# Graph blocks with the state stored points-first: aggregate p before the weights are applied, high parts of p before low parts

## The reference

```python
for i in range(NUM_BLOCKS):                          # 4 blocks
    shortcut = points
    p = _lrelu(points)
    g = _group_point(p, idx_t)                       # the 8 nearest
    c = jnp.einsum('oi,bin->bon', w_center[i], p)
    gn = jnp.einsum('oi,bikn->bokn', w_neighbor[i], g)
    points = (c + gn.sum(axis=2)) / (K + 1.0) + shortcut
...
agg = jnp.einsum('bnkc,bnk->bnc', xk, att)           # 30 nearest, softmax weights
return x + agg.transpose(0, 2, 1)
```

## Time and profile before

| | |
|---|---|
| median of 3 runs | 747.92 us (745.57 to 748.06) |
| profiled execution | 747.99 us, its span 746.1 us |
| TensorE busy | 720.4 us, 97% of the span |
| VectorE, ScalarE, GpSimd busy | 80%, 40%, 35% |
| granted TensorE clock, mean | 0.991 of 2.4 GHz |
| gram stage | 0 to 136.2 us |
| block loop | 136.2 to 614.7 us |
| slots 8 to 15 of the eight iterations begin at | 167.4, 221.2, 272.3, 347.6, 415.1, 466.7, 517.7, 571.3 us |
| attention and last store | 614.7 to 746.1 us |

### The profile page before, as it was taken

The page is one execution under the profiler, slowest core; times in us unless marked ns, Lnnn a source line. Parts: engine busy times, 40 slices in busy tenths (PEclk is TensorE's granted clock), DMA queues, the critical chain, the costliest instruction groups (busy, mean ns, idle before and its releaser), DMA issues.

```text
span 746.1 us, 13230 instructions
## 1 busy us (share of the span) xinstructions
PE 720.4 (97%) x5530; PEld 595.1 (80%) x5530; DVE 596.6 (80%) x884; ACT 302.0 (40%) x505; POOL 258.6 (35%) x207
## 2 busy tenths in 40 slices
PE   6999999969999999999999999999998998999998
PEld 4789888858888887888888788888887886777776
DVE  4699999969799999989977979668566777878731
ACT  7436847536634343113302353563552223333210
POOL 2238986955607327203620460651530000000000
PEclk9999999989999999999999999999999999999999
DMA  9612030020002013464300000000000000001001
GB/s 352 215 2 114 1 114 0 1 113 0 1 19 95 2 67 122 164 212 171 125 2 0 1 1 0 1 1 0 1 0 1 2 1 15 30 30 37 36 29 57
DMA packets 21180, 39.88 MB, mean 53 GB/s; under 512 B 10112, under 2 KB 10112, under 8 KB 20864
## 3 DMA queue, kind: packets, MB, share of 16 engines
q1 hardware_dynamic: 20976, 36.93, 14.2%
q10 hardware_dynamic: 144, 2.10, 0.8%
HBM read 32.59 MB, written 6.42 MB: 52 GB/s over the span
## 4 chain that ended last, share of the span: by engine, by line
PE 83%; DVE 8%; POOL 4%; ACT 2%; issue 2%; DMA 1%; SPq 0%; POOLq 0%; DVEq 0%; ACTq 0%
PE bank L1498 31%; PE bank L1477 7%; PE bank L1478 7%; PE bank L1479 7%; PE bank L1522 5%; PE bank L1632 5%; PE bank L1582 4%; PE bank L1633 4%; PE bank L1634 4%; PE bank L1385 2%; PE bank L1387 2%; PE bank L1386 2%; DVE vals L940 2%; DVE idx L942 1%; POOL more L440 1%
## 5 line engine op out<-in xcount | busy, mean ns | idle before, releaser
L1498 PE MATMUL bank<-nbr,pts_l 128*128 128x512 f32 x1024 | 240.9, 393 | 0.4 <-DVE pts_l L978 0.4
L1498 PEld LDWEIGHTS bank<-nbr,pts_l 128*128 128x128 f32 x1024 | 191.7, 189 | 40.5 <-DVE pts_l L978 0.9
L725 ACT CAST pts_l<-bank 128x512 fp32r<-128x512 f32 x64 | 37.6, 588 | 163.5 <-PE bank L1479 163.4
L1477 PE MATMUL bank<-wT,pts_h 128*128 128x512 f32 x256 | 101.2, 395 | 0.0
L1478 PE MATMUL bank<-wT,pts_h 128*128 128x512 f32 x256 | 99.9, 390 | 0.0
L1479 PE MATMUL bank<-wT,pts_h 128*128 128x512 f32 x256 | 99.8, 390 | 0.0
L483 POOL TENSOR_TENSOR scratch<-scratch,q_all 128x512 f32<-128x512 f32 x32 | 43.5, 1365 | 112.1 <-ACT q_all L711 112.1
L986 DVE SCALAR_TENSOR_TENSOR X<-bank,X 128x512 f32<-128x512 f32 x64 | 44.1, 689 | 45.6 <-PE bank L1498 44.5
L834 ACT CAST nbr<-bank 128x512 fp32r<-128x512 f32 x64 | 37.5, 588 | 99.1 <-PE bank L1582 99.1
L1385 PE MATMUL bank<-pts_h 128*128 128x512 f32 (+2 forms) x192 | 70.0, 364 | 7.4 <-DVE pts_l L918 7.4
L488 POOL TENSOR_TENSOR pts_h<-scratch,pts_h 128x512 fp32r<-128x512 f32 x56 | 76.5, 1371 | 0.0
(11 more groups left out here) (209 smaller groups left out, 1324.4 us busy)
## 6 DMA issues: line engine op xcount, KB each, us to landing
more<-a_rows SPq DMA_DIRECT2D x17, 480.0 KB, 4.0
scratch<-a_rows SPq DMA_DIRECT2D x15, 480.0 KB, 4.3
X<-in_ctx SPq DMA_DIRECT2D x12, 512.0 KB, 7.0
out_dram<-X SPq DMA_DIRECT2D x16, 256.0 KB, 2.0
more<-in_ctx SPq DMA_DIRECT2D x4, 512.0 KB, 7.0
scratch<-in_fside_BxSxS SPq DMA_DIRECT2D x2, 1024.0 KB, 12.6
w_keep<-wT SPq DMA_DIRECT2D x1, 2048.0 KB, 6.9
X<-in_x SPq DMA_DIRECT2D x2, 1024.0 KB, 6.2
```

The source lines that it names most:

```text
L1477: pe.matmul(bank[g % 3][:], p_h[:, t, cols], wT[:, 0, t, :], start=(t == 0), stop=False)
L1498: mm = pe.matmul(bank[3 + g % 3][:], y[:, m, t * P:(t + 1) * P], nbr[b][:, m, hf * HALF:(hf + 1) * HALF], start=(m == 0 and part_ == 0), s ...
```

## The change

The host hands x and `fside` over transposed and the state X is stored with points on the partitions (128 points, 512 channels). With this:

- A block is computed as (A + I) p first, then the weights. Slots 0 to 7 are now `aggregate` (16 matmuls, operands p and `nbr`), evacuated by ACT `q_high` and DVE `q_low`; slots 8 to 15 are `wp` (12 matmuls, q and W), and DVE's `x_update` follows those. The number of matmuls is the same.
- Every aggregation unit runs its 8 products with p_h first, then the 8 with p_l. Unit 0 of an iteration waits for p_h and then for p_l piece by piece.
- The 8 pieces of p for the next iteration are issued in slots 8 to 15 as before. These are now the wp slots, and the first piece waits for the aggregation to end.
- `w_turn` and `turn_x` are gone. The split of W runs from SBUF (ACT `w_high`, POOL `w_low`), the second weights are loaded again at g = 32 instead of kept; the split of X for the attention reads X directly.
- The norms of batch 1 come from the diagonal of its gram blocks (`gram_diagonal`, POOL), so `norms(1)` moves to the end of the gram stage and POOL's `add_norm` of tiles 8 to 13 behind it; 8 squares and 7 adds are gone.
- Gram blocks 3 and 11 take two pieces of 320 columns in place of 256 and 512.
- `STEPS_AT` and `ADJ_AT` are shifted; selection ends at g = 43, lookups, network begin one slot earlier; the spreads still begin at g = 121.
- In `attend` the attention weights are the stationary operand and X is the moving one.

```diff
-    PIECES = [((min(t, 2) * P, HALF, 0), (HALF, N, 1)) if t < 4 else ((min(t, 6) * P, N, 1),) for t in range(NT)]
+    CUTS = (HALF, HALF, HALF, 704)
+    PIECES = [((t * P, CUTS[t], 0), (CUTS[t], N, 1)) if t < 4 else ((min(t, 6) * P, N, 1),) for t in range(NT)]
...
-        ADJ_AT = {4: (8, 9), 8: (10, 11), 11: (12, 13), 14: (14, 15)}
+        ADJ_AT = {3: (8, 9), 6: (10, 11), 8: (12, 13), 12: (14, 15)}
...
+            def gram_diagonal(T):
+                cols = slice((T - NT) * P, (T - NT + 1) * P)
+                pool.wait_ge(s_gc, pieces_done(T))
+                if T == NT:
+                    pool.wait_ge(s_sqmm, NH)
+                pool.affine_select(out=diag_g[:, cols], in_=score[T][:, cols], compare_op=ALU.is_equal, fill=0.0,
+                                   base=0, pattern=[[-1, P]], channel_multiplier=1).then_inc(s_dg, 1)
...
-                if 0 < n < N2 and n % (2 * CT) == 0:
-                    act.wait_ge(s_wm, NT * it)
+                if 0 < n < N2 and m == 0:
+                    act.wait_ge(s_m, 2 * CT * it)
...
             def aggregate(g):
                 it, j = g // (2 * CT), g % (2 * CT)
...
-                for m in range(NT):
-                    if j == 0:
-                        pe.wait_ge(s_yl, NT * it + m + 1)
-                    for part_, y in enumerate((y_h, y_l)):
-                        mm = pe.matmul(bank[3 + g % 3][:], y[:, m, t * P:(t + 1) * P],
+                    pe.wait_ge(s_ql, g - 2)
...
+                for part_, p in enumerate((p_h, p_l)):
+                    for m in range(NT):
+                        if j == 0:
+                            pe.wait_ge(s_p1 if part_ else s_p0, NT * it + m + 1)
+                        mm = pe.matmul(bank[g % 3][:], p[:, m, t * P:(t + 1) * P],
...
+            def wp(g):
+                it, m = g // NT, g % NT
+                hf, cols = m // CT, slice(m % CT * P, (m % CT + 1) * P)
+                hi = 0 if it < 2 else 1
+                if m % CT == 0:
+                    pe.wait_ge(s_ql, 2 * CT * it + CT * (hf + 1))
...
             for it in range(ITS):
+                for j in range(2 * CT):
+                    aggregate(2 * CT * it + j)
+                    side(16 * it + j)
                 for m in range(NT):
-                    if 16 * it + m > S0:
-                        spread(2 * (16 * it + m - S0) - 2)
+                    if 16 * it + NT + m > S0:
+                        spread(2 * (16 * it + NT + m - S0) - 2)
                     wp(NT * it + m)
-                    side(16 * it + m)
-                for j in range(2 * CT):
...
-                    aggregate(2 * CT * it + j)
-                    side(16 * it + NT + j)
+                    side(16 * it + NT + m)
```

477 lines of the change are left out of this document (197 added, 280 removed).

## The result

The changed kernel takes **785.95 us** (median of 4 runs, 783.84 to 789.21), the kernel before 747.89 beside it (745.57 to 748.06): ratio 1.052, 95% interval 1.047 to 1.057. Slower, as forecast, but by 38 us and not by 17, and outside the range of 752 to 778. The profiled execution has a span of 787.4 us (746.1 before) and a mean granted clock of 0.954 (0.991). It is the slowest of the four, so the profile shows 24 us above the forecast where the median is 21 above it.

A forecast was written before the change was run, and what follows sets the result against it. TensorE, busy 97% of the span, was taken as the bound. Removed work -26.0, waits for p +37.5, clock +5.2 and the gram's end +0.5 gave +17.2 on 748.0: 765 us, range 752 to 778.

The forecast's parts named there:

- Waits for p: First aggregation unit of iterations 1, 2, 5, 6, 7: TensorE waits for the chain making p, 37.5 us in all.
- The clock's price: Work behind the five waits for p runs at the low clock: +5.2 us, bounds 0 and 13.
- rival B: The clock stays low longer after each wait, as at the start: +13 instead of +5, 773 us; chance 0.12.
- 2 to 3 and 3 to 4: ... No wait: Changes of iteration beside lookups (slots 45 to 60): lookup pairs in the wp phases cover the chain, no wait for p.
- w_turn -3.3: Removing w_turn's 16 transposes, 1.7 us, twice: -3.3 us.
- gram blocks -2.7: Gram blocks 3 and 11 in pieces of 320 columns: -1.3 us each, -2.7 together.
- Wait at the turns of tiles 8 and 9: TensorE reaches these turns after 5 long units, not 6 short; about 1.2 us of waiting left: -6.4 us.
- Last wp: Iteration 7's wp, paced by VectorE: 8 slots of 3.9 us plus 1.8 to the first unit, 33 us.
- Attention: Attention stage: turn_x gone from 8 units, -4.2 us; contiguous moving operand, matmuls 0.228 us apart, -3.4.
- Rivals C and D: C: loop's start falls behind, +5, 770 us, chance 0.06. D: waits and clock together 25 us, 748, chance 0.10.
- Rival E: p is ready in time at the iteration changes, no wait and no slow clock: 722 us; chance 0.08.

The follow-up runs named there:

- Experiment 5: Changed kernel, POOL's p work of iterations 3 and 4 cut to 16 columns: 771.8 us; kernel before, 16 POOL instructions added after first one-hots in slots 48-55: 751.8.
- experiment 6: own_slots with POOL's two instructions per piece of p waiting, in lookup slots, until VectorE has made both one-hots: 738.8 us.
- old_pieces: The changed kernel with the gram blocks cut as before, nothing else undone: 784.7 us, ratio 1.050.
- own_slots: The changed kernel with each piece of p made in its own place instead of two shared buffers: 749.1 us, ratio 1.0025.
- Experiment 7: The run of old_pieces: the changed kernel with the gram blocks cut as before, 784.7 us.
- best1: own_slots, iteration 4's pieces waiting again for the low part two pieces before, and the attention's one-hots and spreads two slots earlier: 741.6 us, ratio 0.993.
- filler: The changed kernel with 14 more unused matmuls in the first unit of iterations 1, 2, 5, 6 and 7: 780.3 us, ratio 1.043.
- best2: own_slots with POOL waiting for both one-hots in lookup slots, spreads two slots earlier, p prepared ahead where there are no lookups: 730.0 us, ratio 0.979.

## Why the prediction was wrong in size

- **Waits for p: the mechanism right, the sum by luck.** Five changes, none at 2 to 3 and 3 to 4, the releaser, the period of 3.88, the chain's 30.2 us. Four of the five waits were right within 1.0 us. The first was forecast as 10.3 and was 4.2: the chain ended 36.8 us after its phase began (forecast 37.5), but wp 0 took 29.2 us where 21.9 and 2.1 of turns had been counted, since the wait at the turns of tiles 8 and 9 and its slow clock stand in the same phase and cover p as well.
- **The clock's price: mis-sized**, 5.2 us forecast, 12.5 measured (1.7 to 2.9 at each change). It was taken from one row behind which 3 us of work ran slowly; behind these waits it was 3.4 us at the change to iteration 1 (clock 0.52) and about 4 or more at the others (0.50). The rule that the prediction quoted from the Trainium skill ("TensorE: Matmul & The Clock Gate", section "HAM oscillation — how this bites in real kernels"), every change paying in full, is borne out: the two short waits paid 2.4 and 2.9 us. But its 6.5 us used the same price. This is rival B's term of +13, which had a chance of 0.12; the row that B took its price from shows matmuls 0.43 us apart beside a granted clock of 1.00, so that B was near by its number and not by what that row shows. The 7.3 us too few here and the 6.1 and 2.1 too many in the waits cancelled.
- **"2 to 3 and 3 to 4: ... No wait", read as no cost: the step that failed**, +11.6. It looked at TensorE's wait for p, and at what lookups give the chain in cover, and not at what the chain does to the lookups. The rows of before had it: the wp phase with eight pairs of lookups took 40.8 us while POOL was idle. VectorE needs 4.6 of the 5.1 us of such a slot (36.55 / 8) and TensorE all of it; POOL's share of p, in the aggregation slots until then, moved into these short slots, and VectorE's need went beyond them. Experiment 5 took it out (-13.8 us in these slots) and put it into the kernel before (+5.6 us in one phase), and experiment 6 moved it within the slots (-10.4). About half of the loss is waiting and half the lower clock behind the waits. Some 2 of the 11.6 us were not there in old_pieces, whose program is the same in these slots (123.4 us).
- **A part of the same step**: the copy of an index row on ACT now stands behind a piece of p that waits for POOL, and TensorE waited 3.2 us for it (line 1482, releaser line 721). It is gone in own_slots, where wp 2 still took 34.7 us and TensorE waited 3.15 us behind VectorE instead; the copy alone does not set these slots.
- **w_turn -3.3, gram blocks -2.7**: the work went, but 2.8 us came back as a wait for ACT and its slow clock. Experiment 7 shows it for the blocks; for `w_turn` it was not tried.
- **Wait at the turns of tiles 8 and 9**: 3.4 us left where 1.2 were taken; iteration 0 and its change came out 1.0 below the forecast all the same, because that wait covered p's.
- **Last wp, +3.7**: the pace was right, 3.81 us a slot against 3.9. TensorE waits 3.41 us at 630.2 for the first one-hots, which had not been counted beside the 1.8. Two slots earlier, the last aggregation and wp together were 2.6 us shorter (best1).
- **Attention**: matmuls start 0.227 us apart, so the -3.4 are confirmed. The stage gained 5.1 us and not 7.6, since its first 8 us ran at a clock of 0.59. The gaps of 0.8 and 1.4 us there stood before too (0.7 and 1.4, clock 0.79), and in old_pieces the clock stayed at 1.00 behind them and the stage took 120.6 us, the forecast's 121.0. The term was right. The miss is that clock, which own_slots and filler had too (123.4 and 123.5 us).
- **Rivals C and D** did not come true: TensorE was busy for 32.18 of the 32.22 us of the first aggregation, and waits and clock together were 41.8 us, not 25.
- **Rival E** (p in time: 722) is what own_slots made. It took 749; 12.7 of the 27 us are the lookup slots (126.6 against 113.9), which E as costed did not have. With those repaired, the spreads two slots earlier and p prepared ahead (best2), 730.

## What to carry to other kernels

When a step moves between phases, ask two things: who waits for it now, and whom it disturbs while it runs. An engine that is not waited for can still lengthen another's operations, and a phase in which the bound engine and the next one are both nearly full has no room for it; there, let the operations that the bound engine waits for go first. When a sum comes out right, compare its terms one by one: here two errors of 8 and 7 us stood behind a difference of 1. A ring of two buffers behind a chain of three engines sets a period that no engine shows as busy time; writing intermediate values where the results will lie removed it here without any memory.
